# A two-layer model on one core: a front stage whose work for the second to sixth sequence is placed at other tiles

## The chip, the cores and the metric

The kernel runs on one core of a Trainium2 chip. The metric is the device time of one execution in microseconds (us). All times are of that core. Its engines are TensorE (PE; PEld is its loading of stationary operands), VectorE (DVE), ScalarE (ACT), GpSimd (POOL) and SyncE (SP), which only issues transfers. Each engine runs its own list of instructions in order, and they wait for each other on semaphores.

## The reference

Eight sequences of 512 tokens with 128 features go through two layers, each with modulated layer norms. Cut to what matters for the change, the first layer is:

```python
mod = (_silu(L0_c) @ L0_wmod).reshape(L0_c.shape[0], 6, 1, -1)
sa, ca, ga, sb, cb, gb = (mod[:, 0], mod[:, 1], ...)
h = _layernorm(x, axis=-1) * (1 + ca) + sa
x = x + ga * _L0_attn_ref(h, ...)
h = _layernorm(x, axis=-1) * (1 + cb) + sb
x = x + gb * _L0_ffn_ref(h, ...)
# _L0_attn_ref: a linear recurrence over the tokens, then a layer norm
xp = x @ Wp + bp
h = associative_scan(...)            # h[t] = lam * h[t-1] + xp[t] * B
out = (h . C) @ Wo + bo
z = out + x
return layernorm(z) * ln_gamma + ln_beta
# _L0_ffn_ref: _tlin(x, w, s) = (x @ w.T) * s with w of -1, 0, 1
h = silu(_tlin(x, w1)) * _tlin(x, w2)      # 128 -> 512
h = gelu(_tlin(h, h1))                     # 512 -> 512
h = gelu(_tlin(h, h2))                     # 512 -> 512
return _tlin(h, w3)                        # 512 -> 128
```

The second layer has gated linear attention over 8 heads and a feed-forward part with low-rank experts. The change does not touch it.

## The kernel before

`front()` computes the first layer, `linear_attention()` and the code behind it the second. `front()` takes the eight sequences in four pairs (`PAIRS`, index i). A pair is 24 output tiles of 128 features by 512 tokens (`TILES`, index j): j 0 to 7 are the first feed-forward layer (four tiles for each sequence, each a `gate` and an `up` product), j 8 to 15 and 16 to 23 the two hidden layers. Behind tile 23 stands the `y` product of the pair's first sequence; the `y` product of the second stands behind tile 3 of the next pair.

Float32 values are multiplied exactly enough by splitting: a value x is cut into a high part (`hi`, rounded to the short form fp32r) and a low part (`lo` = x - hi), and each is multiplied by the weight. So a gate or up product is two matmuls of 512 columns (L1024, L1025), a layer-0 tile four, a hidden tile eight. The weights are exact in the short form only if their low halves are zero. ScalarE adds the magnitudes of these halves while the weights land (`sum_piece`, one for each of the parts in `PARTS`), TensorE adds them over the partitions (`flag`), VectorE compares the sum with 0 (L633, `w_inexact`), and TensorE loads the result (`value_load`) and branches: one copy of the loop (`run(True)`) uses `w_hi`, which ScalarE rounds in seven pieces (`high_piece(k)`, bounds in `CUTS`), the other the raw weights. Tile 8 of the first pair waits for the fourth piece, tile 16 for the seventh.

While TensorE works on the tiles of one pair, everything that the next pair needs is made between them. For each sequence b the steps are, in this order: `moments_in(b)` (DVE, statistics of x), `rescale_shift(n_in, b)` (POOL, rstd and shift), `normalise(b)` (ACT, four 128x128 operations into `ssm_out`), `flip_h(b)` (PE, four transposes), `bring_h(b)` (ACT, into `ssm_hT`); for a pair `project(p)` (PE), `bring_u(p)` (ACT), `scan(p)` (DVE, the recurrence); then `z(b)` (PE), `moments_out(b)` (DVE), `rescale_shift(n_out, b)` (POOL), `normalise_z(b)` (ACT), `update(b)` and `moments_ffn(b)` (DVE), `rescale(n_ffn, b)` (POOL), `apply_ffn(b)` (DVE, into `ffn_out`), `flip_ffn(b)` (PE), `bring_ffn(b)` (ACT, high part and value of h) and `low_h(b)` (DVE, low part of h). `add_bias(b)` (POOL) adds a term to x, two of them for each pair. `spread(k)` makes a per-sequence vector as wide as a tile; ACT copies it out. For the first two sequences this chain runs ahead of the loop, in `prepare()` of each engine, with `centre` and `update_centred` in the place of `normalise_z` and `update`.

Beside these steps a tile of layer 0 costs ScalarE a silu (`gate`, L808) and the high part of a product (L813), VectorE the product (L590) and the low part (L603); a hidden tile costs ScalarE two gelus (L820, L822), VectorE a low part, for the second hidden layer also a rounding cast (L601). An activation table load stands on ScalarE at each change between silu and gelu.

The order is written by hand: each engine's loop has lines of the form "at this i and j, this step". TensorE writes to 8 banks; tiles take banks 0 to 3 in turn, steps take 4 to 7. `setup_uses()` and `loop_uses()` list who uses which bank in TensorE's order, and `claim` makes TensorE wait until the use before in that bank has been read. Names as flip(4), z(2) or project(1) stand for the step with that number.

The lines of the loop before on TensorE that the change rewrites:

```python
if i == 0 and j in (2, 3): flip_h(claim, j)
if i == 0 and j == 5: project(claim, 1)
if i < 3 and j in (8, 9): z(claim, e + j - 8)
if i == 0 and j in (11, 12): spread(claim, j - 9)
if i < 2 and j == 15: flip_h(claim, e + 2)
if i < 3 and j in (17, 18): flip_ffn(claim, e + j - 17)
if i < 2 and j == 21: flip_h(claim, e + 3)
if i < 2 and j == 23: project(claim, i + 2)
```

## Time and profile before

| | |
|---|---|
| median of 3 runs | 614.51 us |
| the runs | 614.43, 614.51, 618.19 us |
| the profiled execution | 613.57 us, of which the span of the trace is 611.30 |
| granted TensorE clock, mean over the span | 0.95 |
| TensorE matmul busy | 536.6 us (88%), 3740 instructions |
| TensorE weight load busy | 441.5 us (72%) |
| VectorE busy | 405.9 us (66%), 1055 instructions |
| ScalarE busy | 329.8 us (54%), 586 instructions |
| GpSimd busy | 190.6 us (31%), 241 instructions |
| end of the front stage on TensorE | 246.2 us |

Times in the trace are counted from the start of the span. Busy shares are means over three stages with different limits; the change is in the first alone, so its stretches are what to read. A busy matmul engine may still run at half its clock, so the granted clock stands beside the busy time.

### The profile page before, as it was taken

To read this page: it belongs to the slowest core of one execution; us is meant where nothing else is said; L and a number is where in the kernel's file an instruction comes from. 1 tells how busy PE (TensorE), PEld (TensorE's weight loads), DVE (VectorE), ACT (ScalarE), POOL (GpSimd) and SP (SyncE) were. 2 spreads that over 40 slices of the span, in tenths; PEclk is the share of its full clock that TensorE was granted. 3 is DMA by queue.
4 is the path that set the end of the run, shared out by engine and by line. 5 is a ranking of instruction groups with operands and counts; after the bars stand their busy time and mean duration, and the time that the engine had idled before them with its cause. 6 is when DMAs were issued, how large, how long until landed. Compare 5 with 4: busy or idle time off the path is not lost. (4 is left out here: it accounts for less than half of the span.)

```text
span 611.3 us, 10259 instructions
## 1 busy us (share of the span) xinstructions
PE 536.6 (88%) x3740; PEld 441.5 (72%) x3740; DVE 405.9 (66%) x1055; ACT 329.8 (54%) x586; POOL 190.6 (31%) x241
## 2 busy tenths in 40 slices
PE   5499999899989999299999999999998538999994
PEld 3468767776867787188888788888887427778873
DVE  5886967896686655357869696867759343656632
ACT  4878777767656874476555655455642012443340
POOL 3512210340110000334455464627354321223311
PEclk9879999999999999699999999999999867999997
DMA  8400000000050000000000000000000000000101
GB/s 299 121 1 2 1 0 1 1 2 0 1 166 2 0 1 1 1 1 1 2 1 2 1 1 1 4 1 1 1 1 2 1 1 0 19 18 17 35 19 34
DMA packets 10656, 11.66 MB, mean 19 GB/s; under 512 B 720, under 2 KB 9360, under 8 KB 10352
## 3 DMA queue, kind: packets, MB, share of 16 engines
q1 hardware_dynamic: 9552, 10.50, 5.3%
q8 instruction: 30, 0.49, 0.4%
q10 hardware_dynamic: 1056, 0.52, 0.3%
q14 instruction: 18, 0.15, 0.1%
HBM read 8.92 MB, written 2.10 MB: 18 GB/s over the span
## 5 line engine op out<-in xcount | busy, mean ns | idle before, releaser
L1024 PE MATMUL bank<-ffn_g_hi,w_hi 128*128 128x512 f32 x288 | 116.4, 404 | 0.1
L1025 PE MATMUL bank<-ffn_g_lo,w_hi 128*128 128x512 f32 x288 | 113.6, 394 | 0.0
L1269 DVE TENSOR_TENSOR_SCAN att_decay<-bank,att_ident 128x512 f32<-128x512 f32 x64 | 77.6, 1213 | 34.5 <-PE bank L1581 34.3
L603 DVE TENSOR_TENSOR ffn_g_lo<-ffn_full,ffn_g_hi 128x512 fp32r<-128x512 f32 x96 | 66.0, 687 | 29.7 <-ACT ffn_full L822 28.4
L1589 PEld LDWEIGHTS bank<-att_qT,att_hT 128*128 128x128 f32 x512 | 66.0, 191 | 5.5 <-issue 2.0
L1589 PE MATMUL bank<-att_qT,att_hT 128*128 128x128 f32 x512 | 67.9, 276 | 0.6 <-DVE att_state L1293 0.6
L1024 PEld LDWEIGHTS bank<-ffn_g_hi,w_hi 128*128 128x128 f32 x288 | 54.1, 188 | 14.0 <-DVE ffn_g_lo L603 2.2
L1025 PEld LDWEIGHTS bank<-ffn_g_lo,w_hi 128*128 128x128 f32 x288 | 54.1, 188 | 11.8
L1468 ACT COPY att_qT<-bank 128x512 f32<-128x512 f32 x64 | 37.3, 587 | 44.3 <-PE bank L167 41.0
L822 ACT ACTIVATE ffn_full<-bank,cols 128x512 f32<-128x512 f32 x64 | 44.5, 695 | 31.0 <-PE bank L1025 25.0
L1277 DVE TENSOR_TENSOR att_prob<-bank,att_decay 128x512 f32<-128x512 f32 x64 | 42.6, 666 | 21.9 <-issue 20.4
L1371 POOL TENSOR_TENSOR att_vw<-att_v,att_decay 128x128 f32<-128x128 f32 x64 | 25.9, 406 | 69.4 <-DVE att_decay L1269 69.4
L1959 PE MATMUL bank<-l,lora_hid 128*128 128x155 f32 x256 | 35.6, 296 | 0.0
L700 POOL TENSOR_TENSOR ssm_out_rstd<-ssm_out_var,neg_half 128x4 f32<-128x4 f32 x8 | 9.2, 1153 | 84.2 <-DVE ssm_out_var L488 84.2
L1024 PE MATMUL bank<-ffn_h_hi,w_hi 128*128 128x512 f32 x64 | 28.8, 450 | 6.7 <-ACT ffn_gate L808 2.7
L1959 PEld LDWEIGHTS bank<-l,lora_hid 128*128 128x128 f32 x256 | 34.2, 189 | 0.0
L590 DVE SCALAR_TENSOR_TENSOR ffn_full<-bank,cols,ffn_gate 128x512 f32<-128x512 f32 x32 | 23.5, 742 | 13.3 <-ACT ffn_gate L808 12.9
L820 ACT ACTIVATE ffn_g_hi<-bank,cols 128x512 fp32r<-128x512 f32 x32 | 22.5, 704 | 10.9 <-PE bank L1025 10.4
L1837 POOL TENSOR_TENSOR lora_h_lo<-lora_hT,lora_h_hi 128x512 fp32r<-128x512 f32 x8 | 10.2, 1270 | 56.7 <-DVE lora_h_hi L1758 56.7
L1891 ACT CAST lora_zT<-bank 96x512 fp32r<-96x512 f32 x16 | 9.2, 577 | 33.9 <-PE bank L1936 33.9
L165 PE MATMUL bank<-att_h_hi,m_hi 128*128 128x512 f32 x64 | 27.5, 430 | 0.0
L1581 PE MATMUL bank<-att_cut_in,sel 128*128 128x512 f32 x64 | 26.4, 432 | 0.3
(220 smaller groups left out, 1243.0 us busy)
## 6 DMA issues: line engine op xcount, KB each, us to landing
w_raw<-in_w_all SPq DMA_DIRECT2D x2, 1152.0 KB, 10.1
out<-lora_res SPq DMA_DIRECT2D x8, 256.0 KB, 2.3
x<-in_x SPq DMA_DIRECT2D x3, 512.0 KB, 11.9
stage<-in_sel SPq DMA_DIRECT2D x1, 640.0 KB, 8.7
v_raw<-in_v_all SPq DMA_DIRECT2D x1, 576.0 KB, 6.3
x<-in_x ACTq DMA_DIRECT2D x2, 256.0 KB, 3.3
w_raw<-in_w_all SPq DMA_DIRECT2D x1, 512.0 KB, 5.8
gain_attn<-in_WqT SPq DMA_DIRECT2D x1, 512.0 KB, 3.2
```

Source lines behind the costliest of these rows:

```text
L165: pe.matmul(acc, w[0], x[0], start=start, stop=False)
L603: dve.tensor_tensor(lo, full[j % 4][:, :], hi.bitcast(F32), ALU.subtract).then_inc(low, 1)
L822: act.activation(full[j % 4][:, :], ps, ACT.Gelu, scale=scale).then_inc(gelu_ready, 1)
L1024: pe.matmul(acc, w[0], x[0], start=start, stop=False)
L1025: return pe.matmul(acc, w[0], x[1], start=False, stop=stop)
L1269: dve.tensor_tensor_scan(decay[at % ND][:, :], bank("decay", b, k)[:, :], ident4[:, :], 0.0, ALU.mult, ALU.add).then_inc(decay_ready, 1)
L1277: dve.tensor_tensor(prob[k][:, :], bank("score", b, k)[:, :], decay[at % ND][:, :], ALU.mult).then_inc(prob_ready, 1)
L1371: pool.tensor_tensor(vw[s][:, :, hs], v[s][:, :, hs], last.broadcast_to([P, T, DV]), ALU.mult).then_inc(vw_ready, 1)
L1468: act.copy(qT[b % 2][:, k, :], bank("q", b, k)[:, :]).then_inc(q_ready, 1)
L1581: pe.matmul(ps[:, :], r["sel"][:, k, :], cut_in[b % 2][:, :], start=True, stop=True).then_inc(ring_mm, 1)
L1589: mm = pe.matmul(ps[:, cc], hT[s][:, cc], qT[s][:, k, cc], start=True, stop=True)
L1959: mm = pe.matmul(bank_e[s][t // 2][:, at:at + D + AR], hid[s][:, k, t * P:(t + 1) * P], r["war2"][:, k, :], start=(k == 0 and t % 2 == 0), ...
```

## The change

All of it is in `front()`. What it does, engine by engine:

- **Loads.** `PARTS` has four parts instead of three, so the weights come in four transfers and ScalarE adds up four parts. x of sequence 2 is loaded alone, x of 3 behind the last weights; x of 4 and 5 and of 6 and 7 as pairs, as before.
- **TensorE, ahead of the loop.** 22 matmuls of a 128x128 block of ones with itself into bank 7 (`warm`, result unused) stand ahead of the first modulation product, six more behind the two small products. z(1) stands ahead of the second group of modulation products (`vectors(1)`) instead of behind it. The first two tiles of the first pair are written out in `first_tiles()`: four products with the high part of h, then the wait for its low part, then the four with the low part.
- **VectorE, ahead of the loop.** It takes two copies into `cw` and two of `spread` from ScalarE. The comparison with 0 stands ahead of `moments_ffn(0)`, `modulations(2, 8)` behind `apply_ffn(0)`. `moments_in(3)` goes into layer 0 behind j 3.
- **The first pair.** On TensorE flip(2) and flip(3) go from tiles 2 and 3 to 4 and 7, project(1) from 5 to 9, z(2) and z(3) from 8 and 9 to 11 and 12, the two spreads from 11 and 12 to 13 and 14, flip(4) from 15 to 16, the ffn flips from 17 and 18 to 20 and 21, flip(5) from 21 to 23, project(2) out of this pair behind tile 1 of the next. ScalarE's and VectorE's steps move with them.
- **Pairs 1 and 2.** flip(6) from 15 to 16, the ffn flips from 17 and 18 to 18 and 19, flip(7) from 21 to 22, project(3) behind tile 1 of pair 2. `bring_h(5)` and `bring_h(7)` stand behind the first gate of the next pair.
- **GpSimd.** `rescale_shift(n_in, 3)` and `(n_in, 4)` stand behind `rescale(n_ffn, 1)`, and in each pair `rescale_shift(n_out, b)` stands ahead of the two `add_bias`.

The diff, cut to what decides the order:

```diff
-    PARTS = (0, 1024, 3328, WCOLS)
-    PART = (0, 1, 1, 1, 2, 2, 2)
+    PARTS = (0, 1024, 3328, 4864, WCOLS)
+    PART = (0, 1, 1, 1, 2, 2, 3)
...
@@ VectorE, prepare()
+                    for s in slots:
+                        at = slice(s * SD, (s + 1) * SD)
+                        dve.tensor_copy(cw[at, s, :], bank("cw", 0)[at, 0:D]).then_inc(cw_ready, 1)
                     moments_in(2)
...
                     scan(0)
-                    moments_in(3)
+                    for k in range(2):
+                        dve.wait_ge(mm, full_at("spread", k))
+                        dve.tensor_copy(r[SPREAD[k]][:, 0:4, :].rearrange("p b n -> p (b n)"), bank("spread", k)[:, :]).then_inc(spread_ready, 1)
...
@@ VectorE, layer0(i) and the hidden tiles
-                            if j == 6:
-                                scan(1)
+                            if j == 3:
+                                moments_in(3)
...
+                        if i == 0:
+                            if j == 10:
+                                scan(1)
+                            if j == 11:
+                                moments_in(4)
+                            if j in (12, 13):
+                                moments_out(j - 10)
+                            if j in (15, 16):
+                                update(j - 13)
+                            if j in (16, 17):
+                                moments_ffn(j - 14)
+                            if j in (18, 19):
+                                apply_ffn(j - 16)
+                            if j == 20:
+                                moments_in(5)
+                            if j in (21, 22):
+                                low_h(j - 19)
...
@@ GpSimd
+                for b in (3, 4):
+                    rescale_shift(n_in, b)
                 for i in range(3):
                     e = 2 * i + 2
                     for b in (e, e + 1):
+                        rescale_shift(n_out, b)
+                    for b in (e, e + 1):
                         add_bias(b)
-                    for b in (e, e + 1):
-                        rescale_shift(n_out, b)
...
@@ ScalarE, layer0(i) and the hidden tiles
-                            if j in (3, 4):
-                                bring_h(j - 1)
                             if j == 5:
+                                normalise(3)
+                                bring_h(2)
+                            if j == 6:
                                 high_piece(3)
-                            if j == 6:
-                                bring_u(1)
...
+                            if j == 8:
+                                bring_h(3)
+                            if j in (8, 9, 11):
+                                high_piece((8, 9, 11).index(j) + 4)
+                            if j == 10:
+                                bring_u(1)
+                            if j == 13:
+                                normalise(4)
+                            if j in (14, 15):
+                                normalise_z(j - 12)
+                            if j in (15, 16):
+                                spread(j - 13)
+                            if j == 17:
+                                bring_h(4)
+                            if j in (21, 22):
+                                bring_ffn(j - 19)
+                            if j == 22:
+                                normalise(5)
...
@@ TensorE
+                def warm(at, count):
+
+                    for _ in range(count):
+                        pe.matmul(psum[at][:, 0:P], r["ones"][:, :], r["ones"][:, :], start=True, stop=True)
...
+                    def first_tiles():
+
+                        pe.wait_ge(w_high, 1)
+                        pe.wait_ge(ffn_h_high, 1)
+                        accs = []
+                        for j in range(2):
+                            for what, col in (("gate", W1), ("up", W2)):
+                                ps = claim(pe, what, 0, j)
...
+                        pe.wait_ge(h_low, 1)
+                        for ps, weights in accs:
...
```

In the built program the change shows on each engine. The first place is TensorE's start: `scT` and `wmod` are the modulation's operands, `rows` and `cols` small constants, `ssm_out` what a flip transposes. Before:

```order
L969 MATMUL bank<-scT,wmod 128x8 x3
L995 MATMUL bank<-rows 64x128
L999 MATMUL bank<-cols 32x1 x2
L241 MATMUL bank<-cols,ssm_out 128x128 x8
L943 MATMUL bank<-ssm_hT,cols 32x512 x2
L963 MATMUL bank<-cols,spread_col 128x128 x8
```

After:

```order
L1041 MATMUL bank<-ones 128x128 x22
L1018 MATMUL bank<-scT,wmod 128x8 x3
L1051 MATMUL bank<-rows 64x128
L1055 MATMUL bank<-cols 32x1 x2
L1041 MATMUL bank<-ones 128x128 x6
L241 MATMUL bank<-cols,ssm_out 128x128 x8
L992 MATMUL bank<-ssm_hT,cols 32x512 x2
L1012 MATMUL bank<-cols,spread_col 128x128 x8
```

The two groups of matmuls on `ones` are new; the rest stands in the order it had. The second place is VectorE from the statistics of sequence 0's `ffn_in` to the update of sequence 1 (`ssm_out_stats` and `ssm_zn` are sequence 1's). Before:

```order
L479 BN_STATS ffn_in_stats<-x 128x6 x4
L483 BN_AGGR ffn_in_mv<-ffn_in_stats 128x2 x4
L488 TENSOR_SCALAR ffn_in_var<-ffn_in_mv 128x4
L633 TENSOR_SCALAR w_inexact<-bank 1x1
L479 BN_STATS ssm_out_stats<-bank 128x6 x4
L483 BN_AGGR ssm_out_mv<-ssm_out_stats 128x2 x4
L488 TENSOR_SCALAR ssm_out_var<-ssm_out_mv 128x4
L505 TENSOR_SCALAR ffn_out<-x,ffn_in_mv,ffn_in_rstd 128x128 x4
L555 SCALAR_TENSOR_TENSOR ssm_zn<-bank,ssm_out_mv,gain_attn 128x128 x4
L563 SCALAR_TENSOR_TENSOR x<-ssm_zn,ssm_out_rstd,x 128x128 x4
```

After, from the comparison on:

```order
L650 TENSOR_SCALAR w_inexact<-bank 1x1
L494 BN_STATS ffn_in_stats<-x 128x6 x4
L498 BN_AGGR ffn_in_mv<-ffn_in_stats 128x2 x4
L503 TENSOR_SCALAR ffn_in_var<-ffn_in_mv 128x4
L494 BN_STATS ssm_out_stats<-bank 128x6 x4
L498 BN_AGGR ssm_out_mv<-ssm_out_stats 128x2 x4
L503 TENSOR_SCALAR ssm_out_var<-ssm_out_mv 128x4
L520 TENSOR_SCALAR ffn_out<-x,ffn_in_mv,ffn_in_rstd 128x128 x4
L533 TENSOR_SCALAR mod<-bank 128x3x8 x2
L570 SCALAR_TENSOR_TENSOR ssm_zn<-bank,ssm_out_mv,gain_attn 128x128 x4
L578 SCALAR_TENSOR_TENSOR x<-ssm_zn,ssm_out_rstd,x 128x128 x4
```

The comparison now stands ahead of these statistics, and the modulations of `mod` (which stood ahead of the shown rows) between `ffn_out` and `ssm_zn`; the low part of h follows three kinds of row further down in both. The third place is ScalarE in layer 0 of the first pair, from the gate of tile 3 before and of tile 4 after (`ffn_gate` gates, `ffn_g_hi` high parts, `ssm_hT` a `bring_h`, `w_hi` a weight piece). Before:

```order
L808 ACTIVATE ffn_gate<-bank,cols 128x512
L813 CAST ffn_g_hi<-ffn_full 128x512
L762 ACTIVATE ssm_hT<-bank,sa_bo,mod 128x512
L808 ACTIVATE ffn_gate<-bank,cols 128x512
L813 CAST ffn_g_hi<-ffn_full 128x512
L762 ACTIVATE ssm_hT<-bank,sa_bo,mod 128x512
L808 ACTIVATE ffn_gate<-bank,cols 128x512
L813 CAST ffn_g_hi<-ffn_full 128x512
L778 CAST w_hi<-w_raw 128x768
L808 ACTIVATE ffn_gate<-bank,cols 128x512
L813 CAST ffn_g_hi<-ffn_full 128x512
L768 ACTIVATE ssm_u<-bank,b_bias,rows 64x512
```

After:

```order
L847 ACTIVATE ffn_gate<-bank,cols 128x512
L852 CAST ffn_g_hi<-ffn_full 128x512
L789 ACTIVATE ssm_out<-x,ssm_in_shift,ssm_in_rstd 128x128 x4
L801 ACTIVATE ssm_hT<-bank,sa_bo,mod 128x512
L847 ACTIVATE ffn_gate<-bank,cols 128x512
L852 CAST ffn_g_hi<-ffn_full 128x512
L817 CAST w_hi<-w_raw 128x768
L847 ACTIVATE ffn_gate<-bank,cols 128x512
L852 CAST ffn_g_hi<-ffn_full 128x512 x2
L859 ACT_TABLE_LOAD
L859 ACTIVATE ffn_g_hi<-bank,cols 128x512
L861 ACTIVATE ffn_full<-bank,cols 128x512
```

Before, one `bring_h` each stands between gates 4 and 5 and the piece behind high part 4; after, `normalise(3)` (`ssm_out`) and one `bring_h` stand behind high part 4, the piece behind high part 5, and the other `bring_h` only behind the table load and the first gelu.

## Rows read from the trace of the kernel before

**Rows 1.** Sums by stretch, first pair: us, busy (instructions), granted clock, DMA share, GB/s.

```profile
core 0: us, PE busy (x) PEld busy (x) DVE busy (x) ACT busy (x) POOL busy (x), PEclk, DMA share, GB/s
30.90:87.60 56.70, 54.26 (x252) 41.73 (x253) 45.89 (x124) 43.64 (x75) 13.68 (x14) 0.95 0.00 1
```

**Rows 2.** Sums of TensorE's waits, 30.9 to 246: us in total, times, longest.

```profile
PE bank L241 <- ACT ssm_out L750: 4.2, 4, 1.7
```

**Rows 3.** Timeline of TensorE: start, us, instruction, in brackets idle time before and releaser.

```profile
84.15 0.39 PE L1024 MATMUL bank<-ffn_g_hi,w_hi 128*128 128x512 f32 x1
...
84.38 0.39 PE L1025 MATMUL bank<-ffn_g_lo,w_hi 128*128 128x512 f32 x1
...
84.70 1.05 PE L943 MATMUL bank<-ssm_hT,cols 128*32 128x512 f32 x4
...
85.68 0.50 PE L1024 MATMUL bank<-ffn_g_hi,w_hi 128*128 128x512 f32 x1
...
120.55 0.66 PE L241 MATMUL bank<-cols,ssm_out 128*128 128x128 f32 x4 [1.67 <-ACT ssm_out L750]
...
178.68 0.66 PE L241 MATMUL bank<-cols,ffn_out 128*128 128x128 f32 x4 [2.40 <-DVE ffn_out L505]
```

**Rows 4.** Sums by stretch for TensorE alone: us, busy (instructions), granted clock, DMA, GB/s.

```profile
26.00:28.00 2.00, 0.45 (x2) 0.65 0.00 0
31.00:36.00 5.00, 5.00 (x14) 0.50 0.00 0
```

**Rows 5.** Timeline of all engines, layer 0 of the first pair.

```profile
41.19 0.77 ACT L762 ACTIVATE ssm_hT<-bank,sa_bo,mod 128x512 f32<-128x512 f32 x1
...
41.86 0.68 ACT L808 ACTIVATE ffn_gate<-bank,cols 128x512 f32<-128x512 f32 x1
...
42.43 0.61 ACT L813 CAST ffn_g_hi<-ffn_full 128x512 fp32r<-128x512 f32 x1
...
42.57 0.75 DVE L590 SCALAR_TENSOR_TENSOR ffn_full<-bank,cols,ffn_gate 128x512 f32<-128x512 f32 x1
...
42.94 0.84 ACT L778 CAST w_hi<-w_raw 128x768 fp32r<-128x768 f32 x1
...
44.96 0.40 PE L1024 MATMUL bank<-ffn_g_hi,w_hi 128*128 128x512 f32 x1
...
45.75 1.21 DVE L549 TENSOR_TENSOR_SCAN ssm_state<-lam_col,ssm_u 64x512 f32<-64x512 f32 x1
```

**Rows 6.** Timeline of VectorE and ScalarE, end of the first pair.

```profile
73.64 0.87 DVE L479 BATCH_NORM_STATS2 ssm_in_stats<-x 128x6 f32<-128x128 f32 x4
...
78.70 1.64 ACT L750 ACTIVATE ssm_out<-x,ssm_in_shift,ssm_in_rstd 128x128 f32<-128x128 f32 x4
...
80.51 1.78 DVE L578 TENSOR_TENSOR ffn_h_lo<-ffn_h,ffn_h_hi 128x512 fp32r<-128x512 f32 x1
...
88.55 1.28 ACT L808 ACT_TABLE_LOAD   x1
```

**Rows 7.** Timeline of all engines, from the flag to the first tiles.

```profile
21.44 0.29 PE L1015 MATMUL bank<-ones,w_lo_sum 128*1 128x1 f32 x6
...
22.79 0.14 DVE L633 TENSOR_SCALAR w_inexact<-bank 1x1 int32<-1x1 f32 x1
...
27.55 1.08 PE L241 MATMUL bank<-cols,ffn_out 128*128 128x128 f32 x4 [5.82 <-issue]
...
30.15 0.69 DVE L578 TENSOR_TENSOR ffn_h_lo<-ffn_h,ffn_h_hi 128x512 fp32r<-128x512 f32 x1 [0.66 <-ACT ffn_h L247]
...
30.76 3.05 DVE L505 TENSOR_SCALAR ffn_out<-x,ffn_in_mv,ffn_in_rstd 128x128 f32<-128x128 f32 x4
```

**Rows 8.** Timeline of all engines, the start.

```profile
6.35 1.42 PE L969 MATMUL bank<-scT,wmod 128*128 128x8 f32 x6 [6.35 <-DMA wmod<-in_wmod]
...
13.14 2.05 PE L963 MATMUL bank<-cols,spread_col 128*128 128x128 f32 x16
...
13.31 0.77 ACT L768 ACTIVATE ssm_u<-bank,b_bias,rows 64x512 f32<-64x512 f32 x1 [1.50 <-PE bank L943]
```

192 lines of the change are left out of this document (108 added, 84 removed).

## The prediction

> **What bounds the kernel now.** The change touches only the front stage, which TensorE ends at 246.2 us; all behind it stays. The sums by stretch [rows 1] show how the front spends its time: in the first of its four pairs of sequences TensorE is busy 54.26 of 56.70 us (96%), VectorE 45.89 (81%), ScalarE 43.64 (77%). So TensorE's own work bounds a pair, and what can be won is its waits plus the time before its first pair, which starts at 30.9. The sums of waits name the largest group: 4.2 us in four waits for `ssm_out`, which ScalarE's `normalise` brings late [rows 2]; the timeline places the longest of them, 1.67 us, at 120.55, and one of 2.40 for `ffn_out` at 178.68 [rows 3]. I number the 24 tiles of a pair t0 to t23 as the code does; t0 to t7 are layer 0 (four products each), t8 to t23 are hidden tiles (eight each).
>
> Prices that I use, start to start. One 512-column product takes 0.234 at the full clock (84.15 to 84.38) [rows 3], so a hidden tile 1.87, a layer-0 tile 0.93, and at half clock, where 14 products and flips filled 5 us [rows 4], near twice that; a flip of four blocks 0.4 beyond its wait, an estimate from its 0.66 less the overlap [rows 3]. ScalarE: gate 0.57, high part of a product 0.51, weight piece 0.82, `bring_h` 0.67 [rows 5], `bring_ffn` and a hidden tile's two gelus 2 x 0.57 to 0.67 as the same kind, `normalise` 1.64 with 0.1 of overlap, table load 1.28 [rows 6]. VectorE: product 0.75 and scan 1.2 [rows 5], moments 1.5, of which 0.87 is the statistics [rows 6] and 0.6 my estimate for the small operations behind, low part 0.69 [rows 7], product and low part less the 0.1 that neighbours overlap; gates 0.95 as one estimate for six small operations that stand in the same place before and after.
>
> **The change part by part.** All times below are where a step would stand in the changed kernel on the clock of the profiled execution.
>
> Ahead of everything 22 warm-up matmuls start near 1.0. A 128x128 f32 matmul is two passes; 16 such passes took 2.05 at the full clock (0.13 each, 0.11 start to start), so twice that cold [rows 8]. Before, passes ran at half speed from the first matmul at 6.35 until the projection and at full speed from 13.14, 6.8 us later; after 30.9 the clock was still 0.50 at 36.0, over 5 us later [rows 4, 8]. With that delay 12 to 14 of them run cold: 5 to 6 us, the rest 2, so the first real matmul comes at 8.3 to 8.8 instead of 6.35. The clock is then full: `vectors`, the two small products and six more warm-up matmuls (1.3) end at 10.9, and both flips and, behind the second `hT`, the projection take half of what they took cold. `ssm_u` can start at 13.9 instead of 13.31 [rows 8]. Price: +0.6; bounds 0 (clock up after 3.5 us) and +2.7 (never up). VectorE takes the two `cw` copies (under 0.6) and the two spreads (about 0.65 each) while it waits for `ssm_u` and for z(0): nothing, unless z(0) came over 0.6 earlier.
>
> TensorE runs z(0), z(1), vectors(1), flag instead of z(0), vectors(1), z(1), flag: same work, flag at 21.4 + 0.6. The fourth sum costs ScalarE 0.2, but two `cw` and two spread copies have left it, so the sums stay ahead of the flag. The compare moves ahead of `moments_ffn(0)`: 21.75 + 0.6 instead of 22.79: flagged 0.5 earlier. From the flag to the flip took 27.55 - 22.93 = 4.6 us of TensorE's own [rows 7]; it stays, so the flip is at 27.0 and the high part of h at 28.2. Four high products start at 29.0. But the low part waits for VectorE, which now has `moments_ffn(0)`, `moments_out(1)`, `apply`, `modulations`, `centre`, `update`, `moments_ffn(1)` behind the flag: it comes at 30.6 instead of 30.15, the low products at 31.3 to 33.0. So t1 ends at 33.0, not 34.5: 1.5 won. One more thing is won here: `ffn_out` of sequence 1 took 3.05 us with POOL's two adds beside it [rows 7], where ScalarE's `normalise`, the same four operations, takes 1.64 [rows 6]; POOL's adds move behind `rescale_shift` of the second pair, and 1 us or more of it goes.
>
> Now layer 0 of pair 0. Before, the four-bank ring and the half clock held TensorE, and ScalarE put gate 5, high 4, weight piece 3 one after the other at 41.86, 42.43, 42.94 [rows 5], so t8, which waits for that piece, could start at 44.96 right behind t7. In the new order ScalarE has `normalise(3)` and `bring_h(2)` between high 4 and gate 6, and piece 3 only behind high 5. Follow VectorE: product 0 at 32.7, product 1 at 33.5, low 0, low_h(1) until 36.1, product 2, low 1, gates, product 3 until 39.05, low 2, `moments_in(3)` (1.5, new in this place) until 41.15, product 4 until 41.9. ScalarE waits: high 4 until 42.5, then POOL's rstd and shift of sequence 3 (1.0 + 0.2 and their waits, 42.6), `normalise(3)` 44.2, `bring_h(2)` 44.8, gate 6 45.4, high 5 45.9, piece 3 46.8. t8 starts at 46.8 against 44.96: **+1.85**, the 1.5 is gone and more.
>
> From t8 to the y product of pair 0 there were 85.68 - 44.96 = 40.7 us. New in them:
> project(1) behind t9 (50.6) needs `bring_h(3)`, which stands behind product 7, high 7, the table load (49.95) and gelu 8: 51.8, and then 0.98. It takes 2.25; the project(2) that leaves this stretch took 1.07: +1.2.
> scan(1) needs `bring_u(1)`, which stands behind gelu 10: t10 ends 54.7, gelus 56.0, `ssm_u` 56.8, scan 58.0; t11 ended at 56.5, z(2) waits 1.5 where it waited 0.2: +1.3.
> flip(4) behind t16 needs the bank that the copy of spread(2) frees. ScalarE behind t15: 0.2 + 1.15 + `normalise_z(3)` 1.5 + copy 0.6 = 3.45, TensorE is there after 1.87: 1.6 of waiting, as there was before at the same flip (one of the four waits that make 4.2 [rows 2]): 0.
> ffn flip(2) stands behind t20. `update`, moments and `apply` now run between low parts of the third layer, which cost VectorE 1.05 (cast and low part) where second-layer ones cost 0.60: from gelu 16 the chain low 16, update, moments, low 17, moments, low 18, apply is 8.4 us, TensorE's t17 to t20 are 7.5, and gelu 16 is late by 1.6 itself against the un-delayed t16: a wait of 1.2, plus half a collision below (0.2): +1.3.
> flip(5) stands behind t23, its `normalise(5)` behind gelu 22 and `bring_ffn(3)`: 0.2 + 0.57 + 1.32 + 1.54 = 3.7 with 0.3 of lag, t23 is 1.87: waits 1.85 where 0.65 stood: +1.2.
> Together +5.0; the y product is **+6.8** late.
>
> Pair 1, layer 0: project(2) now stands behind t1 and needs `bring_h(5)`, placed behind gate 0. Gate 0 comes 4.1 behind the y product (`bring_y` and the table load, which ended at 89.83; the y product began at 85.68 [rows 3, 6]), `bring_h` until 5.4, project 1.0: t2 at 6.4 instead of 4.9 and t4 at 10.55 instead of 9.4: **+1.15**. The same in pair 2 costs 0.1, since there the 1.07 of the projection leaves the end of the pair in exchange.
>
> What the moves win. Pair 1: flip(6) waited 1.67 [rows 3]; one tile later it has 1.87 more: the whole wait goes, and the ffn flip behind t18 instead of t17 waits as long for `apply` as before, so one tile of 1.87 is won once; flip(7) wins 0.65. Against it: POOL's adds for sequences 4 and 5 ran ahead, one of them near 80.5, in slack; now they follow `rescale_shift(n_out)`, among VectorE's low parts and updates of the same pair. The VectorE operation that met one there took 1.78 instead of 0.69 [rows 6, 7], so an add costs 0 (not met) to 1.1; of two, part falls into VectorE's gaps, and 1.0 is what can reach the flip; I take the middle, 0.5. **-2.0**. Pair 2: the 2.40 wait at 178.68 [rows 3] shrinks by one tile, 1.87, with the same collision 0.5: **-1.4**. Pair 3: nothing.
>
> The lock itself is a rule of the Trainium skill (SBUF — State Buffer, "Who interferes with whom"): GpSimd and VectorE share one pair of ports, and whoever starts first blocks the other for the whole instruction. The trace agrees with its 1.78. Taken at its word each collision is a full add and the three pairs would cost 1.2 more: 620.2.
>
> Sum: 1.85 + 5.0 + 1.15 + 0.1 - 2.0 - 1.4 = +4.7; with 0.1 less, since the start of t8 is rounded up, +4.6. The loads (x 2 alone and x 3 behind the weights, weights in four parts) change nothing: x 2 comes no later alone than it did with x 3, and x 3 is needed only in layer 0. The profiled execution took 613.57 (span 611.30, 2.27 around it), the median of the runs 614.51, 0.94 more. 613.57 + 4.6 = 618.2; on the median 614.51 + 4.6 = **619.1, forecast 619.0**.
>
> **The rivals.** (a) Faster: ScalarE keeps ahead in pair 0. It decides at one place: if weight piece 3 ends by 43.4, t8 starts behind t7 and keeps the 1.5; then ScalarE is 3.4 earlier at gelu 8 and both project(1) and scan(1) fit. That takes away 1.85 + 1.5 and 1.2 + 1.3: 619.0 - 5.85 = 613.2; if the waits at the ffn flip and flip(5) vanish with it (2.5), 610.7, and with the 1.6 at flip(4) and the 0.6 of the warm-up gone too, 608.5. For it: the total of ScalarE's layer-0 work is 13.1 us from gate 0 at 31.9, so 45.0 without any wait. Against it: that is already behind 43.4, and VectorE's product 4 comes behind `moments_in(3)`. Chance 0.17.
> (b) Near balance: t8 is late as summed, but the 5.0 behind it are 0 to 1.3, since ScalarE and VectorE make up their lag in the hidden tiles, where each has 0.5 to 1.2 of slack a tile: 619.0 - 5.0 = 614.0 to 615.3. Chance 0.13.
> (c) Dearer: the warm-up matmuls never raise the clock (+2.1) and every collision is full (+1.4): 622.5, and 624 if the gelu ring is pushed too. Chance 0.10.
> A rule that speaks for (c): the Trainium skill (TensorE: Matmul & The Clock Gate, Part 1) has the clock at half by default and back to half after an idle stretch. Here the row agrees: 0.65 granted as the mean of 26 to 28, 5 us behind the flag matmul at 21.44, and 0.50 from 31 to 36 [rows 4, 7]. The idle stretch between flag and flip is as long in the changed kernel, so the warm-up buys nothing for the products of pair 0.
>
> **How the numbers follow.** Forecast as summed, 616 to 622: 0.60. (a) 0.17, (b) 0.13, (c) 0.10. Within 1% of 614.51 (608.4 to 620.7, about what a measurement of this kernel can tell from no change) lie (b), 0.10 of (a) and 0.40 of the forecast: 0.63. Slower by over 1%: 0.20 of the forecast and (c), 0.30. Faster by over 1%: 0.07, the end of (a), where the gains of pairs 1 and 2 come without their collisions too. The range 611.5 to 623 leaves out half of (a) and half of (c).
>
> **What would show it.** First real matmul at 8 to 9 and `ssm_u` at 13.5 to 14.5; flag 4.6 before the flip; high products near 29, low ones over 2 later; t8 1 to 3 us later than 44.96 and released by `w_hi`; project(1) waiting for ScalarE, z(2) for the scan; flip(5) waiting near 2; no waits at flip(6), flip(7). I am wrong if t8 starts before 44.5, or if the front ends before 246.

## The result, and the profile after

| | before | after |
|---|---|---|
| median of 4 runs | 614.67 us | 623.42 us |
| all runs | 614.43 to 618.19 | 622.97 to 624.11 |
| the profiled execution (span) | 613.57 (611.30) | 624.11 (621.9) |
| TensorE, start of the last `y` product of the front | 242.62 | 250.27 |
| granted clock, mean | 0.954 | 0.944 |

The ratio of the runs is 1.0124, 95% interval 1.0098 to 1.015: slower, by a little over 1%. The forecast was 619.0, slower by 0.7%. The direction was right. That ratio applied to the 614.51 from which the forecast counts gives 622.1, inside its range of 611.5 to 623.0; the median itself, 623.42, lies 0.4 above it. Slower by over 1% had a chance of 0.30.

Time went at two places. The front stage became 7.65 us longer. Behind it the instructions are the same, and yet the two profiled spans differ by 10.6: 2.95 us more.

The sums by stretch of the changed kernel, from its first product to the start of the first tile of pair 1, answer to [rows 1]:

```profile
core 0: us, PE busy (x) PEld busy (x) DVE busy (x) ACT busy (x) POOL busy (x), PEclk, DMA share, GB/s
29.90:95.60 65.70, 55.64 (x248) 41.70 (x249) 45.59 (x142) 44.58 (x78) 12.52 (x15) 0.92 0.00 1
```

The pair took 65.7 us instead of 56.7. VectorE and ScalarE are as busy as before in us (45.6 and 44.6 against 45.9 and 43.6), TensorE 1.4 more: of the 9.0 us, 7.6 are waiting. The sums of TensorE's waits in the front, where [rows 2] stood:

```profile
PE bank L241 <- DVE ffn_out L520: 3.5, 3, 1.7
PE bank L1080 <- DVE ffn_full L605: 2.8, 5, 1.5
PE bank L241 <- ACT ssm_out L789: 2.1, 2, 1.8
PE bank L241 <- ACT gain_attn L813: 1.5, 1, 1.5
PE bank L1080 <- ACT w_hi L817: 1.4, 1, 1.4
PE bank L1001 <- DVE ssm_state L564: 1.4, 1, 1.4
PE bank L992 <- ACT ssm_hT L801: 1.2, 2, 0.6
```

The waits for `w_hi`, `ssm_state` and `gain_attn` are new kinds; the one for `gain_attn` stands at flip(4), which waited 1.50 before, for `ssm_out`. The timeline places them; the lines are a product of tile 6, tile 8, z(2), flip(4), the ffn flip and flip(5) of the first pair, and the ffn flip of pair 2 (compare the last lines of [rows 3]):

```profile
42.50 0.50 PE L1080 MATMUL bank<-ffn_h_hi,w_hi 128*128 128x512 f32 x1 [1.52 <-DVE ffn_full L605]
...
47.43 0.76 PE L1080 MATMUL bank<-ffn_g_hi,w_hi 128*128 128x512 f32 x1 [1.41 <-ACT w_hi L817]
...
59.41 0.49 PE L1001 MATMUL bank<-cols,ssm_hT 128*128 128x128 f32 x2 [1.40 <-DVE ssm_state L564]
...
75.81 0.63 PE L241 MATMUL bank<-cols,ssm_out 128*128 128x128 f32 x4 [1.46 <-ACT gain_attn L813]
...
84.84 0.66 PE L241 MATMUL bank<-cols,ffn_out 128*128 128x128 f32 x4 [0.93 <-DVE ffn_out L520]
...
93.29 0.66 PE L241 MATMUL bank<-cols,ssm_out 128*128 128x128 f32 x4 [1.78 <-ACT ssm_out L789]
...
188.22 0.66 PE L241 MATMUL bank<-cols,ffn_out 128*128 128x128 f32 x4 [1.68 <-DVE ffn_out L520]
```

(The bank of the first was read late, since VectorE did `moments_in(3)` ahead of a product.) Tile starts of the two traces give the difference stretch by stretch, in us, next to the terms of the forecast:

| stretch | forecast | measured |
|---|---|---|
| to tile 8 of the first pair | +1.85 | +2.47 (44.96 to 47.43) |
| tile 8 to the `y` product | +5.0 | +5.55 (85.68 to 93.70, +8.02 in all) |
| `y` product to tile 4 of pair 1 | +1.15 | +1.32 |
| tiles 4 to 23 of pair 1 | -2.0 | -1.19 |
| end of pair 1 to tile 4 of pair 2 | +0.1 | +0.22 |
| the rest of pair 2 | -1.4 | -0.72 |
| pair 3 | 0 | 0 |
| front, with 0.1 off the forecast for rounding | +4.6 | +7.65 |
| behind the front | 0 | +2.95 |

One profile is one execution, and about 1 us of the +7.65 belongs to this one. Two runs below (10 more matmuls behind the front, and GpSimd's adds in pairs 1 and 2) leave every instruction up to the first `y` product as it is in the changed kernel. Their tile 8 came at 46.74 and 46.72, 1.8 behind the kernel before, and their `y` product at 92.64 and 92.62, 6.95 behind it, where the table has 2.47 and 8.02. The front with 10 more matmuls behind it ended at 249.21, 6.6 behind.

### The profile page after: what moved, and what is told of

Same layout as the page of the kernel before. It is cut to its first block and busy times, and to the rows that moved or that the text cites. A ratio compares the mean times of both kernels' runs of the same rounds, so it can differ in the third digit from the quotient of the medians.

```text
span 621.9 us, 10378 instructions
## 1 busy us (share of the span) xinstructions
PE 548.8 (88%) x3798; PEld 452.0 (73%) x3798; DVE 405.7 (65%) x1059; ACT 328.6 (53%) x584; POOL 189.8 (31%) x241
## 5 line engine op out<-in xcount | busy, mean ns | idle before, releaser
L618 DVE TENSOR_TENSOR ffn_g_lo<-ffn_full,ffn_g_hi 128x512 fp32r<-128x512 f32 x96 | 68.2, 710 | 36.7 <-ACT ffn_full L861 35.5
L1080 PE MATMUL bank<-ffn_h_hi,w_hi 128*128 128x512 f32 x60 | 25.9, 431 | 5.1 <-DVE ffn_full L605 2.8
L1919 POOL TENSOR_TENSOR lora_h_lo<-lora_hT,lora_h_hi 128x512 fp32r<-128x512 f32 x8 | 10.2, 1270 | 56.7 <-DVE lora_h_hi L1840 56.7
```

What stands on the lines that cost most here:

```text
L618: dve.tensor_tensor(lo, full[j % 4][:, :], hi.bitcast(F32), ALU.subtract).then_inc(low, 1)
L1080: pe.matmul(acc, w[0], x[0], start=start, stop=False)
```

## The experiments

All edits are to the kernel before or to the changed one, as said; the difference of a front is that of the start of its last `y` product. Two profiles of one kernel can differ at the start: tile 0 came between 28.4 and 32.1 us in the runs below, and between 28.4 and 30.0 in the five profiles that have the changed kernel's start. So tile starts are compared with that in mind; what stood ahead of the edit is named beside the number. The kernel before ran beside them with medians of 615.46 (piece 3, GpSimd's adds, later places alone, delay before), 615.95 (first pair undone, first tiles, both on the warm-up) and 615.96 us (the other four); the ratios are to these.

### Are the moved steps of the first pair the loss?

The changed kernel with every tile step of the first pair back in its old place, and the rest of the change kept. Core of the edit on TensorE; ScalarE, VectorE, GpSimd and the place of the load of x of sequence 3 follow it:

```diff
-                                if j in (4, 7):
-                                    flip_h(claim, 2 + (j == 7))
-                                if j == 9:
+                                if j in (2, 3):
+                                    flip_h(claim, j)
+                                if j == 5:
                                     project(claim, 1)
-                                if j in (11, 12):
-                                    z(claim, j - 9)
+                                if j in (8, 9):
+                                    z(claim, j - 6)
...
```

> The changed kernel with every step of the first pair's tiles back at the tiles of the kernel before (flips, projection 1, z, spreads, pieces, bring_h, scan, moments, updates, ffn flips; x of 3 loaded and normalised early, GpSimd's order for the first pair too). Warm-up, weight parts, the comparison, first_tiles and the new places of pairs 1 and 2 stay. Theory A (the front stage lost 7.65 us: 8.0 in the first pair by its moved steps, 1.3 in layer 0 of pair 1 by the projection, against 1.7 won after it): tile 8 starts at 43.5 to 45.5 instead of 47.43, the y product at 84.5 to 86 instead of 93.7, the front ends at 244.5 to 246.5. Rival (warm-up, parts, comparison or first_tiles cost it): the y product of the first pair stays later than 89.

Measured 613.78 us, ratio 0.9976 (0.9957 to 0.9996); the front's last `y` product at 242.35, 7.9 earlier than in the changed kernel. The `y` product of the first pair came at 87.05 instead of 93.70, which rejects the rival, but tile 8 only at 47.38. So from tile 8 on the steps are the whole loss: 39.7 us from tile 8 to the `y` product, 46.3 in the changed kernel (45.9 in the two other profiles of its first pair). The start up to tile 8 went another way than expected. VectorE now had both `moments_in(3)` and the copies taken from ScalarE ahead of the comparison, which came at 23.91 instead of 22.79 [rows 7], and GpSimd's two adds met `ffn_out` as they do before, 3.04 us:

```profile
23.91 0.14 DVE L651 TENSOR_SCALAR w_inexact<-bank 1x1 int32<-1x1 f32 x1
...
33.58 3.04 DVE L520 TENSOR_SCALAR ffn_out<-x,ffn_in_mv,ffn_in_rstd 128x128 f32<-128x128 f32 x4 [0.91 <-POOL ffn_in_rstd L735]
```

In the changed kernel the same operation took 1.12 at 32.36: that part of the change does what was forecast, but the gain ends at tile 8.

### Why is tile 8 late?

Weight piece 3 ahead of `normalise(3)`, in the changed kernel:

```diff
                             if j == 5:
+                                high_piece(3)
                                 normalise(3)
                                 bring_h(2)
-                            if j == 6:
-                                high_piece(3)
```

> The changed kernel with ScalarE's weight piece 3 put ahead of normalise(3) and bring_h(2) in layer 0 of the first pair. Theory A (the order of ScalarE's steps makes tile 8 late): piece 3 then ends near 44.1 instead of 47.3, so the wait of 1.41 us for w_hi ahead of tile 8 goes; flip(3) behind tile 7 may wait 0 to 1 instead. Tile 8 at 45.5 to 46.5 instead of 47.43, and the front stage ends 1.0 to 2.5 us earlier than the 253.9 of the changed kernel. Theory C (the low clock from 44 to 51 us is the cost, and any late step brings it): tile 8 starts earlier, but tile 8 still takes 3.4 us instead of 1.9, and the gain is under 1.5. Rival (the waits only move): ScalarE is as late at gelu 8 as before, the wait comes back at z(2) (1.40 now, then over 2), and the front ends within 0.5 of 253.9.

Measured 622.8 us, ratio 1.012 (1.0089 to 1.0152). Piece 3 ended at 42.9, the wait for it was gone, tile 8 ran at full clock (1.95 us instead of 3.4), and tile 9 stood 3.1 us ahead of the changed kernel's. One tile later 1.4 was left: project(1) now waited 0.91 for `ssm_hT`, at half of its work:

```profile
44.46 1.00 PE L241 MATMUL bank<-cols,ssm_out 128*128 128x128 f32 x4 [0.21 <-ACT ssm_out L789]
...
49.69 1.05 PE L991 MATMUL bank<-ssm_hT,cols 128*32 128x512 f32 x2
51.64 1.05 PE L991 MATMUL bank<-ssm_hT,cols 128*32 128x512 f32 x2 [0.91 <-ACT ssm_hT L801]
```

Of the 1.4, 0.9 had been there at tile 4 (1.6 at tile 0), ahead of the edit. And the full clock in tile 8 is not the edit's: the two other profiles with the changed kernel's first pair have it too. Against the run with 10 more matmuls, which is the changed kernel up to the end of the front, the front ended 0.4 earlier (248.83 and 249.21). So for the end of the front the rival was right: the wait moves. The place of piece 3 is not what costs; the next thing in ScalarE's row is as late.

All steps of sequence 3 out of layer 0, with those behind it one tile later:

```diff
-                                if j in (4, 7):
-                                    flip_h(claim, 2 + (j == 7))
-                                if j == 9:
+                                if j in (4, 8):
+                                    flip_h(claim, 2 + (j == 8))
+                                if j == 10:
                                     project(claim, 1)
...
-                            if j == 3:
-                                moments_in(3)
```

> The changed kernel with every step of sequence 3 taken out of layer 0 of the first pair: moments_in(3) behind low part 7 on VectorE, normalise(3) ahead of gelu 8 and weight piece 3 behind high part 4 on ScalarE, flip(3) behind tile 8; project(1), bring_u(1), scan(1), z(2), z(3), the spreads, flip(4) and the ffn flips one tile later. Theory A (tile 8 is late by moments_in(3) ahead of product 4 and by normalise(3) ahead of piece 3): the waits of 1.52 and 1.41 us go, tile 8 starts at 43.5 to 45.0 instead of 47.43. The y product of the first pair gains less, since the chain behind is one tile later: 0 to 3. Rival (the half clock and the bank ring hold layer 0 whatever stands there): tile 8 later than 46.5.

Measured 626.5 us, ratio 1.0168 (1.0136 to 1.0199). Tile 8 started at 43.41, 4.0 us earlier than in the changed kernel, of which 0.4 (at tiles 2 to 4) to 0.8 (at tile 0) came from the start: `moments_in(3)` on VectorE and `normalise(3)` on ScalarE do hold up tile 8. But flip(3) waited 5.74 us right behind it, and z(2) still 2.13:

```profile
51.25 1.12 PE L241 MATMUL bank<-cols,ssm_out 128*128 128x128 f32 x4 [5.74 <-ACT ssm_out L789]
...
65.17 0.49 PE L1000 MATMUL bank<-cols,ssm_hT 128*128 128x128 f32 x2 [2.13 <-DVE ssm_state L564]
```

In the wait of 5.74 the clock was halved (0.98 from 48 to 50 us, 0.50 from 50 to 56), so tile 9 took 3.6 instead of 1.9. The front ended 5.4 later than in the changed kernel. I had expected the `y` product of the first pair to gain 0 to 3 and was wrong: I had counted ScalarE's step, and not that `moments_in(3)`, GpSimd's rstd and `normalise(3)` follow each other, 1.5 + 1.2 + 1.5 us, while TensorE has one tile of 1.9 to do. The chain of sequence 3 costs more the further back it goes.

### Warm-up and first tiles alone

```diff
+                    pe.wait_ge(ones_set, 1)
+                    warm(7, 22)
                     pe.wait_ge(silu_ready, 1)
...
+                    warm(7, 6)
```

> The kernel before with the 28 warm-up matmuls alone. By my sum the first real matmul comes at 8.3 to 8.8 and the flag 0.6 later, so the front ends 0.6 later, median +0.6, bounds 0 and 2.7. Rival (the later flag is hidden, or the faster clock gives more back): within 0.3 of the kernel before at tile 0.

Measured 616.13 us, ratio 1.0018 (1.0 to 1.0035), which is 0 to 2.2 us. The first real matmul came at 7.78, tile 0 0.24 later and tile 8 0.13 later. The other way round, in the changed kernel:

```diff
-                    warm(7, 22)
...
-                    warm(7, 6)
```

> The changed kernel without the 28 warm-up matmuls. If they cost 0.6, tile 0 starts 0.3 to 0.9 earlier than 29.96 and the front ends 0.3 to 0.9 earlier. Rival (z and the modulations at half clock lengthen the chain to the flag): tile 0 0 to 2 us later, since z(1) now stands ahead of the second group of modulation products and the flag behind both.

Measured 620.9, ratio 1.0093 (1.0059 to 1.0126), against 1.0124 (1.0098 to 1.015) with them: the intervals overlap. Tile 0 was 0.34 earlier, the front 0.65. These differences are no larger than those between profiles with the same start: the 22 matmuls took 6.71 to 7.67 us in the seven profiles that have them, and without them the front ended at 249.62, between the 249.21 and 250.27 of two profiles with them. So the warm-up gains nothing that can be seen; a cost near the forecast +0.6 fits, and is not measured more closely than the 0 to 2.2 above.

The comparison ahead of `moments_ffn(0)` and `first_tiles()` in the kernel before:

```diff
-                    moments_ffn(0)
                     dve.wait_ge(mm, full_at("flag", 0))
...
+                    moments_ffn(0)
...
                     flip_ffn(claim, 0)
-                    pe.wait_ge(w_high, 1)
+                    first_tiles()
...
```

> The kernel before with first_tiles and the comparison ahead of moments_ffn(0) alone. Theory A (my forecast won 1.5 us at tile 1 by these two): tile 0 starts 0.5 to 1.2 earlier than 30.94, tile 2 1.0 to 1.5 earlier than 35.2, but tile 8 waits for weight piece 3, which ended at 43.8, so it starts 0.3 to 1.2 earlier and the front ends that much earlier: the median falls by 0 to 1.2. Rival (ScalarE is the bound from gate 0 on and starts no earlier): tile 8 within 0.2 of 44.96, no difference.

Measured 615.93, ratio 0.9995 (0.9974 to 1.0016). Tile 0 1.02 earlier, tile 4 1.03, tile 8 0.18: the gain is taken back inside tile 5, where a product waited 1.03 us for VectorE to read its bank and 0.38 before, and the front ends 0.16 earlier. That is what the rival said.

### What the moves win in pairs 1 and 2, and GpSimd's adds

In the changed kernel, the adds of pairs 1 and 2 back ahead of `rescale_shift(n_out)`:

```diff
                     for b in (e, e + 1):
-                        rescale_shift(n_out, b)
+                        (add_bias if i else lambda b: rescale_shift(n_out, b))(b)
                     for b in (e, e + 1):
-                        add_bias(b)
+                        (add_bias if not i else lambda b: rescale_shift(n_out, b))(b)
```

> The changed kernel with GpSimd's two add_bias put back ahead of rescale_shift(n_out) in pairs 1 and 2 (not in the first). Theory A (the adds meet VectorE's low parts and updates; in pair 2 two such operations took 1.28 and 1.78 us instead of 0.69): the waits of 0.90 at flip_ffn in pair 1 and 1.7 in pair 2 fall to about 0.0 and 0.5, and the front ends 1.5 to 2.5 us earlier. Rival (the flip waits for the chain of updates and moments whatever GpSimd does): those waits stay within 0.3 of what they are, and the front ends within 0.5 of the changed kernel.

Measured 618.67 us, ratio 1.0061 (1.0043 to 1.0079): 4.75 faster than the changed kernel, or 3.9 by the two ratios to the kernel before. The front ended 3.55 earlier, 1.1 of it ahead of tile 10 of the first pair, where the edit changes nothing, 1.3 in pair 1 and 1.15 in pair 2. In the changed kernel GpSimd and VectorE met like this in pair 2 (GpSimd's two adds; a low part and the first step of `update`, each 0.69 otherwise):

```profile
176.81 2.99 POOL L751 TENSOR_TENSOR x<-x,bias_attn 128x512 f32<-128x512 f32 x2
...
177.36 1.28 DVE L618 TENSOR_TENSOR ffn_g_lo<-ffn_full,ffn_g_hi 128x512 fp32r<-128x512 f32 x1 [1.65 <-ACT ffn_full L861]
178.57 1.78 DVE L585 TENSOR_TENSOR ssm_zn<-ssm_zn,gain_attn 128x512 f32<-128x512 f32 x1
```

The two operations lost 1.69 us to the adds. With the adds back, VectorE stood still 0.47 us in that chain, for a gelu, so 1.2 of the 1.69 could reach the flip, and 1.15 did. In pair 1 two operations lost 2.11, with 0.64 of gaps, and 1.3 came back. The ffn flip of pair 2 waited 0.54 where it had waited 1.68:

```profile
184.67 0.66 PE L241 MATMUL bank<-cols,ffn_out 128*128 128x128 f32 x4 [0.54 <-DVE ffn_out L520]
```

The later places alone, in the kernel before (`late` is 1 in pairs 1 and 2, 0 in the first; ScalarE's `bring_ffn` and VectorE's `low_h` follow):

```diff
+                            late = i > 0
-                            if i < 2 and j == 15:
+                            if i < 2 and j == 15 + late:
                                 flip_h(claim, e + 2)
-                            if i < 3 and j in (17, 18):
-                                flip_ffn(claim, e + j - 17)
-                            if i < 2 and j == 21:
+                            if i < 3 and j in (17 + late, 18 + late):
+                                flip_ffn(claim, e + j - 17 - late)
+                            if i < 2 and j == 21 + late:
                                 flip_h(claim, e + 3)
```

> The kernel before with one part of the change alone: in pairs 1 and 2 flip(6) from tile 15 to 16, the two ffn flips from 17 and 18 to 18 and 19, flip(7) from 21 to 22, and bring_ffn and low_h one tile later; projections and GpSimd's order as before. Theory A: the wait of 1.67 at flip(6) and of 2.40 at the ffn flip of pair 2 shrink to 0 and about 0.5, so the front ends 3 to 4 us earlier than 246.2, near 242.7, and the median falls to 610 to 612 unless the clock of later stages changes. Rival (a flip that is one tile later makes the chain behind it late by as much): the front ends 0 to 1 us earlier, with a new wait at tile 0 of pairs 2 and 3.

Measured 611.48 us, ratio 0.993 (0.9909 to 0.995): faster than before. The front ended 4.54 earlier, 0.3 of it from the start, 2.4 in pair 1 and 1.9 in pair 2. The longest waits of [rows 3] are gone or small:

```profile
120.34 0.62 PE L241 MATMUL bank<-cols,ssm_out 128*128 128x128 f32 x4
...
176.04 0.66 PE L241 MATMUL bank<-cols,ffn_out 128*128 128x128 f32 x4 [0.53 <-DVE ffn_out L506]
```

The flips of the first pair too, in the same kernel:

```diff
-                            if i < 2 and j == 15 + late:
+                            if i < 2 and j == 16:
...
-                            if i < 2 and j == 21 + late:
+                            if i < 2 and j == 22:
```

> The kernel before with flip(4) and flip(6) from tile 15 to 16, flip(5) and flip(7) from 21 to 22, and the ffn flips of pairs 1 and 2 one tile later (as in the run with pairs 1 and 2 alone, and now the flips of the first pair too). Theory A: the waits of 1.50 and 0.49 in the first pair go as well, so the front ends 1.5 to 2.0 us earlier than the 241.7 of that run, the median at 609 to 610.5. Rival (the bank of spread(2) or bring_h(5) behind a later flip(5) takes the gain): within 0.5 of that run.

Measured 608.88 us, ratio 0.9888 (0.9862 to 0.9914), the fastest found together with the next. Its profile stood 1.0 us behind the other at tile 8 and 0.6 ahead at the end of the front, so the two flips gave 1.6. The waits that they had in the first pair of the kernel before are gone:

```profile
67.20 0.66 PE L241 MATMUL bank<-cols,ssm_out 128*128 128x128 f32 x4 [1.50 <-ACT ssm_out L750]
...
80.40 0.65 PE L241 MATMUL bank<-cols,ssm_out 128*128 128x128 f32 x4 [0.49 <-ACT ssm_out L750]
```

And to that kernel the edit of the first tiles and of the comparison:

```diff
-                    pe.wait_ge(w_high, 1)
+                    first_tiles()
...
```

> The same with first_tiles and the comparison ahead of moments_ffn(0). By the run with these two alone they gain 0.2 us: the median within 0.5 of the run without them. Rival (the later flips leave ScalarE room in layer 0, so that the early start lives on): 1 us less.

Measured 609.23 us, ratio 0.9899 (0.9869 to 0.9929): no difference to the run without them, as the run with the two alone had it.

### What happened behind the front

Unused matmuls behind the front, in the kernel before:

```diff
                     y(PAIRS - 1, 1)
+                    warm(7, 33)
```

> The kernel before with 33 unused 128x128 matmuls on ones behind the last y product of the front stage; nothing else is changed, so all later stages run the same instructions, about 7.4 us later. Theory C (the 2.95 us that the changed kernel lost behind the front stage are granted clock, by where its stalls fall): everything behind comes 7.4 us later and the span grows by another 0 to 3.5, and wherever the distance grows, the sums by stretch show 0.50 beside the same instructions that had 1.00. Rival (the later loss is work or a wait that the change brought with it): the span grows by 7.4 and no more, with the same clock by stretch as before.

Measured 622.34 us, ratio 1.0117 (1.0077 to 1.0158). Attention started 8.48 later, and the span grew by 8.7. Behind the delay no clock was lost, so by itself this run fits the rival too. Of the 8.48, 1.5 arose ahead of the edit: at the ffn flip of pair 2, with the same instructions and the same wait as before, the clock was 0.50 in this run, as shown for another at the end of this section.

And fewer of them, in the changed kernel:

```diff
                     y(PAIRS - 1, 1)
+                    warm(7, 10)
```

> The changed kernel with 10 unused 128x128 matmuls behind the last y product of the front, so that all behind comes 2.3 us later and is otherwise the same. Theory C (what the changed kernel lost behind the front is granted clock and hangs on where its stalls fall): in the profile the 1.5 us at the stall of 2.18 near 484 may be absent, and the median then rises by less than 2.3, by 0.5 to 2. Rival (that loss belongs to the changed kernel's work): the median rises by 2.3 and the dip is there.

Measured 622.51 us, ratio 1.0119 (1.0078 to 1.0159): with 10 more matmuls it is no slower than the changed kernel (623.42, ratio 1.0124), and its profiled span is 1.6 shorter (620.3). From the first flip of attention to the end of the span there are 356.6 us in the kernel before, 359.5 in the changed one and 357.2 in the delayed one, so 2.4 of the 2.9 are gone. One place is in the last part of attention, ahead of which TensorE waits 2.2 us in every kernel. The sums by stretch at that place, the changed kernel, then the delayed one:

```profile
483.00:485.00 2.00, 1.07 (x6) 0.79 0.00 0
485.00:487.00 2.00, 2.00 (x11) 0.50 0.00 0
487.00:489.00 2.00, 2.00 (x15) 0.86 0.00 0
```

```profile
483.30:485.30 2.00, 1.58 (x14) 1.00 0.03 8
485.30:487.30 2.00, 2.00 (x16) 1.00 0.00 0
```

And the matmuls themselves (16 of L1718 take 3.55 or 2.02), in the timelines of the changed kernel, of the delayed one, and of the kernel before, where it is L1636:

```profile
483.93 3.55 PE L1718 MATMUL bank<-att_wo,att_outer 128*128 128x128 f32 x16 [2.18 <-issue]
487.28 1.20 PE L1671 MATMUL bank<-att_qT,att_hT 128*128 128x128 f32 x8
```

```profile
483.72 2.02 PE L1719 MATMUL bank<-att_wo,att_outer 128*128 128x128 f32 x16 [2.17 <-issue]
485.58 1.06 PE L1672 MATMUL bank<-att_qT,att_hT 128*128 128x128 f32 x8
```

```profile
474.98 2.02 PE L1636 MATMUL bank<-att_wo,att_outer 128*128 128x128 f32 x16 [2.18 <-issue]
476.84 1.06 PE L1589 MATMUL bank<-att_qT,att_hT 128*128 128x128 f32 x8
```

The same wait and the same 16 matmuls: once the clock was granted, once halved, 1.5 us apart. It was halved there in the profiles of the changed kernel and of the one with piece 3 ahead, in none of the other twelve. The other part, 1.3 us, is at the start of attention, where the clock rose later behind a wait of 8.5 us in both: 8 to 10 us behind the first flip it was still at half in the changed kernel, first line, and full in the kernel before, second line, and in the delayed one.

```profile
270.36:272.36 2.00, 2.00 (x6) 0.50 0.00 0
```

```profile
262.69:264.69 2.00, 2.00 (x10) 1.00 0.00 0
```

The run with the warm-up alone showed the same in the front: the wait of 2.40 ahead of the ffn flip of pair 2 [rows 3] is there to the hundredth, and behind it the flip took 1.11 instead of 0.66 and the front lost 1.5 us:

```profile
178.83 1.11 PE L241 MATMUL bank<-cols,ffn_out 128*128 128x128 f32 x4 [2.40 <-DVE ffn_out L505]
```

```profile
179.00:181.00 2.00, 2.00 (x7) 0.50 1.03 320
```

## Why the prediction was right or wrong

**What bounds: right.** TensorE's own work in the front is the same but for the clock, and the change is worth its waits. It adds waits in the first pair and takes them away in the next two.

**To tile 8: right.** The forecast followed VectorE's product 4 to 41.9 and ScalarE's piece 3 to 46.8; they ended at 42.4 and 47.3, and at 46.6 in the run with 10 more matmuls, where tile 8 is 1.8 late for the forecast 1.85. The 0.6 by which the profile of the changed kernel is off is in the start: the stretch from the comparison to the flip, of which the prediction said that its 4.6 "stays", took 5.07 there (22.89 to 27.96), 4.43 in that run and up to 6.0 in others. The 1.5 us of `first_tiles` were 1.0 at tile 0 and spent by tile 8, in the changed kernel and alone. A wait of 1.52 ahead of a product of tile 6, which I had not listed, is in both of these profiles and is part of how they were spent.

**Tile 8 to the `y` product: right.** z(2) waited 1.40 (forecast 1.5), flip(4) 1.46 (1.6), the ffn flip 0.93 (1.2), flip(5) 1.78 (1.85). Only project(1) did not wait in this profile, since TensorE came to it late: the clock was at half from 44 to 51 us, and tile 8 took 3.4 us instead of 1.9:

```profile
44.00:51.00 7.00, 5.59 (x15) 0.52 0.00 1
```

It fell ahead of the wait for `w_hi`, which began at 46.0, and not in it. TensorE had by then stood still three times, 0.87, 0.56 and 1.52 us, the last up to 42.50:

```profile
43.00:44.00 1.00, 0.94 (x4) 0.92 0.00 0
44.00:45.00 1.00, 1.00 (x3) 0.50 0.02 8
46.00:47.00 1.00, 0.02 (x1) 0.50 0.00 0
```

That the clock was still at half in tile 8 is luck of this profile and not set by the change. The run with 10 more matmuls has the same instructions and the same waits here; its clock fell and was back before tile 8, and the second half of project(1) waited:

```profile
43.00:44.00 1.00, 1.00 (x3) 0.50 0.00 0
44.00:45.00 1.00, 1.00 (x5) 0.50 0.02 8
45.00:46.00 1.00, 0.33 (x2) 0.59 0.00 0
46.00:47.00 1.00, 0.26 (x1) 1.00 0.00 0
```

```profile
46.74 0.47 PE L1080 MATMUL bank<-ffn_g_hi,w_hi 128*128 128x512 f32 x1 [1.41 <-ACT w_hi L817]
...
51.97 1.04 PE L992 MATMUL bank<-ssm_hT,cols 128*32 128x512 f32 x2 [0.30 <-ACT ssm_hT L801]
```

There project(1) took 2.32 from 50.62 on, for the 2.25 from 50.6 of the forecast, and tile 8 to the `y` product is 5.2 longer than before, for 5.0. I had said that rival (a) decides at piece 3 ending by 43.4. That was wrong: it ended at 42.9 in the run with piece 3 ahead and the front won next to nothing, since `bring_h(3)` holds project(1) all the same.

**The projection in layer 0: right**, 1.32 for 1.15 and 0.22 for 0.1.

**The gains of pairs 1 and 2: the step that was mis-sized.** The gains themselves were right: the later places alone won 2.4 and 1.9 in the kernel before, for 2.5 and 1.9 ahead of the deduction. The forecast then took off 0.5 for GpSimd's adds in each pair, the middle of 0 and 1.0. Putting them back gained 1.3 and 1.15: over the top of the bounds. That is 1.45 of the 1.5 by which the two terms were off. The row of the kernel before with 1.78 instead of 0.69 [rows 6, 7] was the price; the middle was too low, because in each pair two of VectorE's operations were met, together 2.1 and 1.7 us longer, and its chain to `ffn_out` had gaps of only 0.64 and 0.47 there. The prediction's own estimate by the rule of the Trainium skill (SBUF — State Buffer, "Who interferes with whom"), that the port pair which GpSimd and VectorE share is locked exclusively, was 620.2, nearer than my 619.0. The trace agrees with the rule for the two operations shown, both with two inputs in SBUF: 1.28 and 1.78 beside two adds of 1.5 each. (The prediction prices full collisions at 1.2 there and at 1.4 in rival (c); by its own terms, 0.5, 0.5 and 0.2, it is 1.2.)

**Warm-up: small, as forecast**, and not measured more closely than that: the first real matmul came at 7.6 to 8.5 where 8.3 to 8.8 was expected, and by the medians the cost is 0 to 2.2 us. The clock was at half again from 24 to 32 us in the changed kernel, and in the run without the warm-up too, so the first tiles began at half clock in both.

**Behind the front: not in the forecast at all.** "All behind it stays" holds for instructions, not for time. 2.8 of the 2.95 us of the profiled difference stand at two places where the granted clock differs and the instructions do not, and 2.4 were gone in the run with 10 more matmuls. In the medians, 8.75 apart, 1.1 is left for it beside this profile's front (8.75 - 7.65), and 2.2 beside the front of 6.6 that the delayed run had. What makes the clock fall behind one wait and not behind the same wait in another run was not found.

So the forecast of +4.5 falls short of the 8.75 by nearly half. 1.45 of that is GpSimd's adds, a term with too low a price. The rest was found, in the profiles, mostly in the granted clock and the start; the prediction has no term for either, and its range had room for them without naming them, which is luck.

## What to carry to other kernels

When steps are moved back along a full engine, look at which of them had waits ahead: those that TensorE waited for won 1.6 to 2.4 us in each pair by one tile. In the same change stood the first pair's moves of many steps that it had not waited for, and as a whole they cost 6.2 to 6.6 us from tile 8 on. A chain of steps over four engines has a length of its own; a step can go back only as far as the chain behind it has room. Where operations of two engines slow each other, price each meeting at its full measured length, less only the gaps that the chain behind it has.

## What the runs showed of the hardware

The clock that is granted behind a wait is not a property of the wait. 2.18 us of idle time ahead of the 16 matmuls of L1718 left it at 1.00 in twelve profiles and at 0.50 in two. 2.40 ahead of the ffn flip of pair 2 left it at 1.00 in two profiles (the kernel before, the first tiles alone) and at 0.50 in two (the warm-up alone, the delay before). Each time it cost 1.5 us; kernels that differ by such an event show it as a difference in time though the change is elsewhere. At the start of the kernel the granted clock reads 1.00 while the warm-up matmuls, 44 passes, took 7.67 us (0.17 each) where 16 take 2.05 later (0.13): the record of the clock does not show the slow start there, the durations do. Two adds on GpSimd, 1.5 us each, made two VectorE operations of 0.69 take 1.28 and 1.78.
